# New place tables for a software-pipelined two-layer kernel on one core

## The chip, the core and the metric

The kernel runs on one core of a Trainium2 chip. TensorE (PE), VectorE (DVE), ScalarE (ACT) and GpSimd (POOL) each work through an instruction list of their own, in order; SyncE (SP) issues most DMAs. The metric is the device time of one execution in microseconds (us), lower is better. It is taken as the median of several executions.

## The reference, cut to what matters

The input is `x` of shape 8 x 512 x 128 in float32: eight batch elements ("batches") that don't depend on each other. Two layers follow each other.

```
xn = layernorm(x)
s  = attention(xn)                       # diagonal masked, softmax over 512
g  = silu(top-2-of-8 experts(xn))        # every expert: 128 -> 256 -> 128
x  = x + s * g
xn = layernorm(x)
s  = mamba(xn)                           # in_proj, conv of 4 taps, selective scan:
                                         #   16 states x 256 channels x 512 steps, out_proj, + xn
g  = silu(sublayer of the nearest of 8 centroids(xn))   # 128 -> 512 -> 128, relu
x  = x + s * g
```

## The kernel before, in words

**Groups of work.** The work of one batch is cut into steps of six groups, named by a letter, a name and a number:

- `A`: the first layer. `ln0`/`xn`/`xT` normalise and transpose; `gl` and `gate` choose the experts; `q k v s p o` are attention (`s0` to `s3` are the score tiles, `p0` to `p3` the transposed probabilities, `o0` to `o3` the outputs); `h0` to `h15` and `m0` to `m7` are the first and second products of the eight experts; `silu` ends the layer.
- `H`: the head of the second layer. `ln1`/`xm`, `hT`, `x1T`, `xi0/1`, `z0/1`, `u`, `bc` (with `bm`, `bl`, `cw`), `sc`, `al`, `rk`, `dl0/1`, `ln`, `du0/1`, and `put0` to `put3`, four indirect DMAs that sort the tokens by expert.
- `S`: the scan. It has 32 scans of 128 x 512 (16 states x 2 halves). `d` is the decay factor on ACT, `b` the spread of a row of B on PE, `scan` the product with B and the scan on DVE, `p` the product with C on POOL, `c` the load of a row of C. `a` adds the states of the first half on PE, `e` those of the second half on POOL (on PE for the last batch), `q` adds two states on DVE (line 1347).
- `F`: the experts of the second layer on eleven token tiles. `w` loads weights, `xs0` to `xs2` transpose, `h0` to `h10` and `y0` to `y10` are the two products, `st` stores, `get0` to `get3` gather back, `ft` and `silu` end it.
- `C`: the end of the batch: `y`, `op` (out_proj), `xr`, `out`.
- `P`: preparation of weights, once. `P pe 0` (lines 957 to 968) is 64 small matmuls.

**Which batch a step works on.** One iteration of the pipeline holds the 32 scans of one batch b. In the same iteration stand the `A` steps of batch b+2, the `H` steps of batch b+1, the `S` and `F` steps of batch b and the `C` steps of batch b-1 (`AHEAD`, line 360). The first layers of batches 0 and 1 and the head of batch 0 have no scans beside them: they fill the pipeline, and their places stand in a table of their own, `OWN` (lines 334 to 352).

**What sets the order.** No engine chooses. Each row of `ROWS` (line 66 on) is `(group, name, number, place, lag on ACT, lag on DVE, lag on POOL, PSUM bank)`. The place is a fraction of the iteration. `place` (line 370) adds the batch; `PLACES` and `ORDER` (lines 376, 377) sort all steps of all batches by it. `program` (line 380) gives each engine its list: PE and SP take the steps by place; ACT, DVE and POOL sort them by `floor(place * 32) + lag`. For DVE the scans are added at 0, 1, 2 ... 31 of their iteration. Steps in `OWN` have no lag. Each engine then runs those parts of a step that are its own.

**What ties the engines.** Semaphores, counted from `ORDER`. Those that matter here:

- `spread` (line 894): PE's `b_n` writes one of two PSUM rows, and waits for scan 2n-3; DVE's product for scan 2n waits for `b_n`, and stands in DVE's list ahead of scan 2n-1 (line 1375 on, `do`).
- Four PSUM banks (`work0` to `work3`) are shared by all products of `A`, `H`, `F` and `C`; `bank_free` (line 595) makes PE wait until the last user of the bank is read out.
- A scan writes one of five state buffers (`STATES`, line 44) and waits until its user before it is added up: in the first half by PE (`a`), in the second by POOL (`e`). `C y` (line 1349) waits for both sums.
- POOL's `get0` (line 1499 on) waits until the last store `st2` of `F` has landed. POOL's `ft` waits for ACT's `ft`.
- `cw` (line 687 on) stores the rows of C, after ACT's `bc`; SP stands still until then.
- ACT's `xn` needs the small POOL instructions of `ln0` (lines 1464 to 1467); PE's `xT` needs `xn`.

`a3`, `a7` and `a11` hold no instruction (their states are added in pairs).

Of the kernel before, what the change touches and what calls it, by code (L numbers as in the profile page):

```python
# [59 lines left out]
def group_tiles(k):  # L60
# [6 lines left out]
    ("P", "dve", 0, -4.19033, 0, 8, 3, None),  # L67
    ("P", "dve", 1, -2.47062, -4, 8, 3, None),
    ("P", "pe", 0, -1.67656, 0, 3, 3, None),
    ("P", "act", 0, -2.74339, 6, -2, -3, None),  # L70
    ("P", "dve", 2, -0.97742, -3, 8, -2, None),
    ("P", "dve", 3, -0.62565, -4, 8, 0, None),
    ("P", "dve", 4, -0.41210, -4, 8, 6, None),
    ("S", "d", 0, -0.06930, 2, -4, 8, None),
    ("S", "d", 1, -0.04250, 2, 4, 8, None),
    ("S", "b", 0, -0.04257, 4, 1, 1, None),
    ("C", "xr", 0, 0.10215, -2, 7, 0, None),
    ("A", "xin", 0, 0.00614, 6, 1, -3, None),
    ("F", "w", 0, 0.03213, -2, 7, 7, None),
    ("F", "xs", 0, 0.00000, 0, 4, -2, 1),  # L80
    ("S", "c", 0, 0.08107, 4, 7, -1, None),
    ("S", "c", 1, 0.10585, 3, 4, -1, None),
    ("F", "w", 1, 0.05645, -3, 0, 3, None),
    ("F", "h", 0, 0.03067, 0, 4, -4, 2),
    ("F", "w", 2, 0.11223, -3, 7, 6, None),
    ("F", "h", 1, 0.05851, 0, 0, -2, 3),
    ("F", "w", 3, 0.25246, 4, 8, 7, None),
    ("S", "d", 2, -0.00699, 1, 0, 8, None),
    ("S", "b", 1, 0.05502, 3, 0, 2, None),
    ("A", "xT", 0, 0.07492, -1, 3, 4, 0),  # L90
    ("S", "p", 0, 0.08069, 7, 8, -2, None),
    ("S", "d", 3, 0.00622, 0, 5, 8, None),
    ("A", "ln0", 0, 0.07442, 2, -3, -2, None),
    ("A", "xn", 0, 0.05034, -1, -3, 2, None),
    ("F", "ld", 1, 0.04079, -4, 0, -1, None),
    ("S", "c", 2, 0.11537, 5, -2, -2, None),
    ("A", "gl", 0, 0.08531, 0, 0, 7, 3),
    ("S", "p", 1, 0.08911, 5, 8, -2, None),
    ("S", "d", 4, 0.08095, -1, -1, 5, None),
    ("S", "b", 2, 0.08914, 4, 4, -4, None),  # L100
    ("C", "y", 0, 0.05655, -1, -1, -4, None),
    ("F", "w", 4, 0.25276, 0, 7, 8, None),
    ("F", "w", 5, 0.42886, -4, 7, 3, None),
    ("S", "p", 2, 0.10331, -2, 7, -1, None),
    ("S", "d", 5, 0.09590, -1, 3, 8, None),
    ("S", "e", 0, 0.10043, -4, -2, -2, None),
    ("A", "q", 0, 0.10060, -1, 4, -4, 0),
    ("C", "op", 0, 0.10037, -4, 0, 2, 1),
    ("A", "k", 0, 0.12863, 0, 6, 3, 3),
    ("A", "gate", 0, 0.10347, 2, 0, 7, None),  # L110
    ("F", "y", 0, 0.08472, 1, 5, 6, 2),
    ("S", "p", 3, 0.11413, 3, 8, -1, None),
    ("S", "d", 6, 0.11844, -1, 7, 7, None),
    ("S", "b", 3, 0.13684, 1, -2, -4, None),
    ("S", "a", 0, 0.06344, 2, -4, 5, None),
    ("F", "y", 1, 0.14612, 0, 3, 6, 3),
    ("C", "out", 0, 0.28650, 0, 8, 8, None),
    ("S", "c", 3, 0.22057, 5, 3, 2, None),
    ("F", "xs", 1, 0.02653, 0, 4, -3, 1),
    ("F", "h", 2, 0.14593, 0, -2, -1, 2),  # L120
    ("A", "s", 0, 0.14700, 0, -1, -2, 0),
    ("S", "p", 4, 0.15628, 1, 8, -3, None),
    ("S", "d", 7, 0.14633, 1, 3, 4, None),
    ("S", "e", 1, 0.15765, -4, -2, -2, None),
    ("F", "w", 6, 0.53888, -1, 7, 7, None),
    ("A", "s", 1, 0.15497, 2, 0, -3, 1),
    ("A", "gT", 0, 0.18211, 0, 6, 7, 2),
    ("A", "s", 2, 0.15828, 1, -1, -1, 3),
    ("A", "s", 3, 0.18212, 1, -1, 6, 0),
    ("S", "p", 5, 0.15952, 6, 8, -2, None),  # L130
    ("S", "d", 8, 0.18533, 1, 2, 6, None),
    ("S", "b", 4, 0.24697, 3, 3, -4, None),
    ("S", "a", 1, 0.13035, 0, -4, -1, None),
    ("A", "v", 0, 0.18227, -2, 1, -2, 2),
    ("A", "p", 0, 0.21815, 1, 7, -3, 1),
    ("F", "st", 0, 0.54576, 2, -1, 5, None),
    ("A", "p", 1, 0.22130, 1, 6, 2, 3),
    ("A", "p", 2, 0.22290, 1, 4, 0, 0),
    ("S", "p", 6, 0.19112, 4, 8, 0, None),
    ("S", "d", 9, 0.23616, 2, 3, 8, None),  # L140
    ("S", "e", 2, 0.25193, -4, -3, -1, None),
    ("S", "c", 4, 0.28439, 5, 6, 2, None),
    ("H", "ln1", 0, 0.25486, -1, 0, 0, None),
    ("H", "xm", 0, 0.33938, -1, -2, -3, None),
    ("A", "p", 3, 0.24715, 1, 4, 0, 2),
    ("A", "h", 0, 0.23766, 1, -4, -4, 1),
    ("A", "h", 1, 0.24707, 1, -1, 1, 0),
    ("S", "p", 7, 0.19307, -1, 8, 2, None),
    ("S", "d", 10, 0.25172, 1, -2, 7, None),
    ("S", "b", 5, 0.25269, 7, 8, 2, None),  # L150
    ("S", "a", 2, 0.20060, 0, -4, 3, None),
    ("F", "h", 3, 0.25384, 0, 3, -3, 3),
    ("F", "y", 2, 0.27707, 0, 7, 3, 0),
    ("A", "o", 0, 0.28591, -1, -3, -2, None),
    ("A", "o", 1, 0.31004, 4, 0, 7, None),
    ("A", "o", 2, 0.32685, 7, 2, 8, None),
    ("A", "o", 3, 0.34065, -1, 3, 1, 2),
    ("H", "hT", 0, 0.36348, 0, 6, 7, 2),
    ("S", "p", 8, 0.25598, 5, 8, 2, None),
    ("S", "d", 11, 0.28789, 0, -1, 7, None),  # L160
    ("S", "e", 3, 0.29700, -4, 0, 0, None),
    ("S", "c", 5, 0.35244, 7, 2, 5, None),
    ("A", "h", 2, 0.25171, 0, -1, -4, 0),
    ("A", "h", 3, 0.32603, -1, -2, -3, 3),
    ("S", "p", 9, 0.25913, 2, 7, 2, None),
    ("S", "d", 12, 0.33869, -1, 5, 3, None),
    ("S", "b", 6, 0.32732, 7, 4, -1, None),
    ("S", "a", 3, 0.39654, 6, -4, 2, None),
    ("A", "b2", 0, 0.25141, 0, 8, -3, 1),
    ("F", "h", 4, 0.27884, 1, -1, -4, 1),  # L170
    ("S", "p", 10, 0.32296, 6, 8, 3, None),
    ("S", "d", 13, 0.37771, -2, 7, 8, None),
    ("S", "e", 4, 0.33495, -4, -3, 0, None),
    ("H", "x1T", 0, 0.46354, -1, 7, -3, 1),
    ("A", "m", 0, 0.33671, 8, 1, 3, 0),
    ("S", "c", 6, 0.38581, 8, 4, 1, None),
    ("S", "p", 11, 0.36266, 5, 8, 2, None),
    ("S", "d", 14, 0.38317, -1, 5, 8, None),
    ("S", "b", 7, 0.35088, 6, 3, -1, None),
    ("S", "q", 4, 0.32753, 3, 1, 6, None),  # L180
    ("S", "a", 4, 0.39944, -1, -3, 6, None),
    ("A", "h", 4, 0.35391, 0, -4, -2, 1),
    ("A", "m", 1, 0.38008, 6, 1, -2, 1),
    ("A", "h", 5, 0.36890, 0, 0, 1, 0),
    ("A", "h", 6, 0.38782, -1, -3, -1, 0),
    ("F", "y", 3, 0.34764, 0, 5, 2, 3),
# [12 lines left out]
    ("S", "b", 8, 0.41835, 6, 5, 4, None),
    ("S", "a", 5, 0.47672, 3, -4, 0, None),  # L200
    ("F", "y", 4, 0.42082, 0, 5, 3, 0),
    ("H", "u", 0, 0.46438, -3, 0, -1, None),
    ("H", "z", 0, 0.52712, -1, 1, 3, 0),
    ("F", "ld", 2, 0.53904, -3, 4, -4, None),
    ("A", "h", 8, 0.50748, -2, 3, -2, 1),
    ("S", "p", 14, 0.43190, 4, 8, 2, None),
    ("S", "d", 17, 0.49706, -2, 0, 8, None),
    ("S", "e", 6, 0.51017, -4, 1, -3, None),
    ("F", "h", 6, 0.49976, -2, 1, -2, 0),
    ("H", "xi", 1, 0.47760, -2, 1, 4, 2),  # L210
# [12 lines left out]
    ("H", "u", 1, 0.53186, -2, 0, 8, None),
    ("A", "m", 3, 0.54082, 8, 2, 3, 1),
# [1380 lines left out]
```

## Time and profile before

| what | value |
|---|---|
| median of 3 executions | 950.92 us (949.97 to 953.21) |
| span of the profiled execution | 950.8 us, 15737 instructions; its device time is not listed apart from this span |
| busy: PE, DVE, ACT, POOL | 831.6, 798.4, 629.8, 604.9 us |
| weight loads of PE | 575.2 us |
| mean granted TensorE clock | 0.951 of full speed |
| first scan, last scan on DVE | start at 133.4 us, start at 932.7 us |

Busy time is the union of an engine's instructions. Matmul ends are modelled, so successive matmuls overlap a little in the rows. "Idle before" is the time in which the engine stood still ahead of an instruction, and the name behind the arrow is what ended it. The windows below are cut at the start of the first scan of each batch.

### The profile page before, as it was taken

How to read it: one execution, taken by the hardware profiler on the slowest of the kernel's cores; microseconds unless marked ns; L12 is line 12 of the kernel's file. 1: busy time of each engine (PE TensorE's matmuls, PEld its weight loads, DVE VectorE, ACT ScalarE, POOL GpSimd, SP SyncE). 2: the span in 40 equal slices, each digit the busy share in tenths (PEclk: the TensorE clock that was granted, in tenths of full speed). 3: DMA queues.
4: the chain of work that ended last, by engine and by line, in shares of the span. 5: the costliest groups of instructions: out<-in, count | busy, mean ns of one | idle time of the engine just before them, and what ended most of it. 6: DMA issues, size and time to landing. Idle time of an engine off the chain costs nothing.

```text
span 950.8 us, 15737 instructions
## 1 busy us (share of the span) xinstructions
PE 831.6 (87%) x4576; PEld 575.2 (61%) x4576; DVE 798.4 (84%) x1503; ACT 629.8 (66%) x1379; POOL 604.9 (64%) x556
## 2 busy tenths in 40 slices
PE   4989999998899879998799869998899876866885
PEld 2767666764677547765576547765676644543552
DVE  3352678999889998999989998899899999998994
ACT  2534667777687856776687866776686865684561
POOL 0000125769585884769585885769585888788664
PEclk9997999999899989999999999999899998886998
DMA  7200122232332333232331333232331333343441
GB/s 261 101 1 1 47 73 85 75 114 78 119 98 77 110 108 82 77 109 80 118 103 68 103 118 84 81 103 86 108 108 62 106 113 107 105 110 103 149 128 38
DMA packets 79430, 90.29 MB, mean 95 GB/s; under 512 B 8450, under 2 KB 49906, under 8 KB 78834
## 3 DMA queue, kind: packets, MB, share of 16 engines
q1 hardware_dynamic: 77298, 85.07, 29.4%
q0 software_dynamic: 2048, 4.20, 1.5%
q8 instruction: 40, 0.66, 0.3%
q14 instruction: 44, 0.36, 0.1%
HBM read 52.96 MB, written 13.04 MB: 69 GB/s over the span
## 4 chain that ended last, share of the span: by engine, by line
PE 39%; DVE 38%; issue 11%; POOL 6%; ACT 5%; SPq 1%; DVEq 0%; DMA 0%; POOLq 0%; ACTq 0%
DVE st L1341 13%; PE work L849 7%; PE work L855 6%; DVE acc L1225 4%; DVE b_row L1328 3%; PE work L890 3%; PE work L880 3%; PE work L778 3%; DVE cv L1254 3%; DVE dbu L1328 3%; POOL st L1518 2%; PE yacc L919 2%; DVE st L1347 2%; ACT prob L975 1%; PE work L769 1%
## 5 line engine op out<-in xcount | busy, mean ns | idle before, releaser
L1518 POOL TENSOR_TENSOR st<-st,Cs 128x512 f32<-128x512 f32 x249 | 320.0, 1297 | 158.0 <-DVE st L1341 152.8
L975 ACT ACTIVATE dA<-delta,Aneg 128x512 f32<-128x512 f32 x256 | 177.7, 718 | 12.9 <-DVE st L1341 12.8
L1341 DVE TENSOR_TENSOR_SCAN st<-dA,b_row 128x512 f32<-128x512 f32 x123 | 148.8, 1210 | 8.0 <-ACT dA L975 7.8
L1341 DVE TENSOR_TENSOR_SCAN st<-dA,dbu 128x512 f32<-128x512 f32 x128 | 154.6, 1208 | 0.0
L1525 POOL TENSOR_TENSOR y<-y,st 128x512 f32<-128x512 f32 x105 | 138.1, 1315 | 3.8
L849 PE MATMUL work<-xnT,w_w1a 128*128 128x512 f32 x256 | 132.7, 612 | 8.5 <-DVE delta L1309 7.0
L855 PEld LDWEIGHTS work<-w_w2a,hid 128*128 128x128 f32 x1024 | 125.1, 196 | 23.4 <-issue 8.7
L919 PE MATMUL yacc<-st,w_ident 128*128 128x512 f32 x208 | 115.7, 641 | 21.9 <-POOL st L1518 16.5
L975 ACT ACTIVATE hsT<-work,hs 128x128 f32<-128x128 f32 x352 | 100.2, 370 | 46.5 <-PE work L880 45.9
L855 PE MATMUL work<-w_w2a,hid 128*128 128x128 f32 x1024 | 128.8, 280 | 0.7 <-ACT hid L975 0.6
L880 PEld LDWEIGHTS work<-xsT,hs 128*128 128x128 f32 x704 | 98.6, 207 | 25.1 <-issue 5.9
L975 ACT ACTIVATE hid<-work,w_b1a 128x512 f32<-128x512 f32 x128 | 86.2, 683 | 37.6 <-PE work L849 33.3
L880 PE MATMUL work<-xsT,hs 128*128 128x128 f32 x704 | 103.2, 294 | 2.6 <-ACT ys L975 1.4
L1225 DVE SCALAR_TENSOR_TENSOR acc<-work,gates,acc 128x128 f32<-128x128 f32 x256 | 71.3, 340 | 35.2 <-PE work L855 32.8
L890 PE MATMUL work<-w_w2f,hsT 128*128 x704 | 99.2, 284 | 0.0
L1328 DVE TENSOR_TENSOR dbu<-b_row,du 128x512 f32<-128x512 f32 x123 | 85.1, 692 | 13.2 <-PE b_row L903 5.9
L890 PEld LDWEIGHTS work<-w_w2f,hsT 128*128 128x128 f32 x704 | 86.0, 192 | 5.7 <-issue 3.0
L1328 DVE TENSOR_TENSOR b_row<-b_row,du 128x512 f32<-128x512 f32 x123 | 84.0, 683 | 2.7
L849 PEld LDWEIGHTS work<-xnT,w_w1a 128*128 128x128 f32 x256 | 43.4, 192 | 42.3 <-issue 17.1
L919 PEld LDWEIGHTS yacc<-st,w_ident 128*128 128x128 f32 x208 | 37.0, 202 | 52.7 <-POOL st L1518 25.4
L1488 POOL DMA_INDIRECT xs_dram<-xn_tok,pos x32 | 32.2, 1006 | 57.6 <-DVE pos L1303 51.2
L903 PE MATMUL b_row<-bc,sel_b 96*128 96x512 bf16 x123 | 48.5, 394 | 21.9 <-DVE st L1341 21.9
(191 smaller groups left out, 1290.9 us busy)
## 6 DMA issues: line engine op xcount, KB each, us to landing
Cs<-c_dram SPq DMA_DIRECT2D x128, 256.0 KB, 3.6
hs<-w_w1f SPq DMA_DIRECT2D x88, 258.0 KB, 2.3
xs_in<-xs_dram SPq DMA_DIRECT2D x16, 256.0 KB, 3.4
ys_dram<-ys SPq DMA_DIRECT2D x16, 256.0 KB, 2.9
w_w1f<-in_w1f_dram SPq DMA_DIRECT2D x1, 2064.0 KB, 8.0
x_in<-in_x_dram SPq DMA_DIRECT2D x8, 256.0 KB, 5.6
w_w2f<-in_w2f_dram SPq DMA_DIRECT2D x1, 2048.0 KB, 12.4
kept_dram<-x_tok SPq DMA_DIRECT2D x8, 256.0 KB, 4.0
```

The lines of the kernel that those rows point to most:

```text
L849: last = mm(w[:], W["w1a"][:, i * 128:(i + 1) * 128], xnT[:], start=True, stop=True)
L855: last = mm(w[:, t * 128:(t + 1) * 128], hid[:, c % 4, t * 128:(t + 1) * 128], W["w2a"][:, c * 128:(c + 1) * 128], start=(c == PER * i), s ...
L880: last = mm(w[:, c * 128:(c + 1) * 128], w1s[:, i % 2, c * 128:(c + 1) * 128], xsT[:, i // 4 % 2, i % 4 * 128:(i % 4 + 1) * 128], start=Tr ...
L890: last = mm(r, hsT[:, i % 2, c * 128:(c + 1) * 128], W["w2f"][:, bass.ds(e * H1 + c * 128, 128)], start=False, stop=(c == HC - 1))
L903: mm(rows_bank(n, b)[:], row_of(n), bc3[:, par], start=True, stop=True).then_inc(sig["B_in"], 1)
L919: mm(yacc[:], ident[:], state(s), start=False, stop=(n == NS - 1)).then_inc(sig["y_sum0"], 1)
L975: return nc.scalar.activation(out, in_, func, **k)
L1225: last = V.scalar_tensor_tensor(acc[:, t], w[:, t * 128:(t + 1) * 128], gates[:, t, i:i + 1], acc[:, t], ALU.mult, ALU.add)
L1328: V.tensor_tensor((dbu0, rows_bank(n, b))[h][:], rows_bank(n, b)[:], du[:, par, h], ALU.mult).then_inc(sig["dBu"], 1)
L1341: V.tensor_tensor_scan(state(s), dA[:, s % DECAYS], (dbu0, rows_bank(n, b))[h][:], 0.0, ALU.mult, ALU.add).then_inc(sig["scan"], 1)
L1518: G.tensor_tensor(state(s), state(s), Cs[:, b.of(NS, n) % C_BUFS], ALU.mult).then_inc(sig["P"], 1)
L1525: G.tensor_tensor(y1[:], y1[:], state(s), ALU.add).then_inc(sig["y_sum1"], 1)
```

## The change

No instruction is added, removed or altered. The places of `ROWS`, its lags and banks, and the tables `OWN` and `OWN_BANKS` have new values. `AHEAD`, `LAG`, `STATES` and all code stay. The diff replaces nearly every row; here are the rows that are spoken of below.

```diff
 ROWS = [
-    ("P", "pe", 0, -1.67656, 0, 3, 3, None),
+    ("P", "pe", 0, -1.91080, 0, 3, 3, None),
...
-    ("F", "xs", 0, 0.00000, 0, 4, -2, 1),
+    ("F", "xs", 0, -0.11627, -2, 4, -2, 3),
...
-    ("F", "h", 0, 0.03067, 0, 4, -4, 2),
+    ("F", "h", 0, -0.02332, 0, 4, -4, 0),
...
-    ("A", "xT", 0, 0.07492, -1, 3, 4, 0),
+    ("A", "xT", 0, -0.00752, 1, 3, 4, 3),
...
-    ("A", "ln0", 0, 0.07442, 2, -3, -2, None),
-    ("A", "xn", 0, 0.05034, -1, -3, 2, None),
+    ("A", "ln0", 0, 0.02507, 2, -10, -5, None),
+    ("A", "xn", 0, -0.07075, 2, -3, 2, None),
...
-    ("C", "y", 0, 0.05655, -1, -1, -4, None),
+    ("C", "y", 0, 0.04106, -1, 0, -4, None),
...
-    ("S", "d", 9, 0.23616, 2, 3, 8, None),
+    ("S", "d", 9, 0.25211, -1, 3, 8, None),
...
-    ("A", "m", 0, 0.33671, 8, 1, 3, 0),
+    ("A", "m", 0, 0.35005, 8, -1, 3, 2),
...
-    ("S", "c", 10, 0.67012, 7, 8, 2, None),
+    ("S", "c", 10, 0.57540, 7, 8, 2, None),
...
-    ("H", "cw", 0, 0.77328, 4, 7, -4, None),
+    ("H", "cw", 0, 0.44605, 4, 7, -4, None),
...
-    ("F", "get", 0, 0.83381, 4, 6, 2, None),
+    ("F", "get", 0, 0.78844, 4, 6, 1, None),
...
-    ("F", "get", 3, 0.88365, 0, 8, 2, None),
+    ("F", "get", 3, 0.93264, 0, 8, 2, None),
...
-    ("A", "m", 7, 0.95782, 8, 0, 4, 3),
+    ("A", "m", 7, 0.97159, 8, -1, 4, 2),
...
 OWN = {
     ("A", 0): (
-        -2.47358, -4.12153, -4.15752, -4.47547, -3.96000, -3.84171, -3.57697, -3.77930, -3.40151, -3.32920, -3.31868, -3.31571,
+        -4.73497, -6.29962, -9.23557, -6.95863, -5.61949, -4.96893, -4.95574, -4.56186, -4.38585, -4.36247, -3.73522, -3.37503,
...
 OWN_BANKS = {
```

What the tables make of the engines' lists, in an iteration in the middle, around the change of batch (the batch is given as an offset from the one whose scans run; the instructions are the same):

```
PE before:   b15 h12..h14(+2) a12 h15(+2) a13 m6(+2) | b0 m7(+1) a14(-1) xs0 a15(-1) xs1 Fh0 b1 Fh1 a0 xT(+2) y0 gl(+2) b2 op(-1) ...
PE after:    b15 h13(+2) xs0(+1) m6(+2) h14 h15(+2) a13 m7(+2) Fh0(+1) | b0 xT(+2) a14 a15(-1) b1 Fh1 y0 b2 gl(+2) xs1 op(-1) ...
DVE before:  scan27 q12 du0 du1 scan28 al scan29 scan30 m6 m7 scan31 ln0(+3) | scan0 silu(+1) Cy(-1) scan1 scan2 ...
DVE after:   scan22 ln0(+3) ... q12 scan27 du0 du1 scan28 m6 scan29 scan30 m7 scan31 | scan0 silu(+1) scan1 Cy(-1) scan2 ...
POOL before: e12 p27 e13 get0 du0 du1 get1 get2 get3 p28 p29 p30 p31 ft e14 e15 ln0(+3) | p0 ...
POOL after:  e12 get0 get1 ln0(+3) get2 du0 du1 p27 p28 e13 p29 p30 e14 get3 p31 e15 ft | p0 ...
SP before:   ... st1 w10 cw c12 c13 c14 st2 c15
SP after:    ... w8 cw c10 xin(+3) c11 keep w9 w10 st1 c12 c13 w0(+1) c14 w1(+1) fetch st2 ld1(+1) c15
```

Further in the iteration: PE before has `b5 Fh3 y2 Fh4 o0 o1 h3 o2 b6 m0`, after it has `b5 y2 Fh4 y3 h2 o0 b6 h3 m0`. DVE before takes `m0` after scan 11, after the change it takes it after scan 10. ACT before has `d8 p0 p1 p2 h0 h1 p3 b2 h2 Fh3 y2 d9`, after it has `p0 p1 h1 d8 p2 d9 Fh3 b2`.

In the fill (batches 0 and 1), ahead of the first `b0` on PE, the list now also holds `h15` and `m6` of batch 1 and `xs0` and `h0` of `F`, 0.86 to 1.79 us each in the rows below. DVE's `ln1` of batch 0 now stands ahead of `gl` and `gate` of batch 1, and ACT's `xm` of batch 0 ahead of the score tiles `s0` to `s3` of batch 1.

## Rows read from the trace of the kernel before

**Rows 1.** The page: span, busy time by engine, and two groups of DVE.
```profile
span 950.8 us, 15737 instructions
PE 831.6 (87%) x4576; PEld 575.2 (61%) x4576; DVE 798.4 (84%) x1503; ACT 629.8 (66%) x1379; POOL 604.9 (64%) x556
...
L1341 DVE TENSOR_TENSOR_SCAN st<-dA,b_row 128x512 f32<-128x512 f32 x123 | 148.8, 1210 | 8.0 <-ACT dA L975 7.8
...
L1328 DVE TENSOR_TENSOR b_row<-b_row,du 128x512 f32<-128x512 f32 x123 | 84.0, 683 | 2.7
```

**Rows 2.** Windows from first scan to first scan: length, busy, clock, DMA.
```profile
0.00:133.42 133.42, 115.78 (x611) 81.09 (x611) 60.25 (x206) 64.71 (x123) 14.45 (x28) 0.95 0.23 76
133.42:239.04 105.62, 97.78 (x562) 67.40 (x560) 97.01 (x188) 79.04 (x175) 72.52 (x67) 0.98 0.32 97
...
345.79:454.74 108.95, 99.87 (x560) 70.01 (x560) 97.94 (x185) 78.17 (x172) 78.30 (x72) 0.95 0.32 94
...
669.60:774.93 105.33, 97.32 (x560) 69.25 (x560) 96.89 (x177) 77.53 (x172) 77.00 (x71) 0.97 0.30 92
774.93:867.31 92.38, 64.70 (x299) 41.67 (x299) 86.48 (x123) 56.45 (x128) 73.92 (x67) 0.82 0.37 106
867.31:950.80 83.49, 64.53 (x308) 40.42 (x306) 65.77 (x79) 39.34 (x98) 53.93 (x43) 0.93 0.37 113
```

**Rows 3.** Waits of DVE, 239.04 to 774.93 us: us, times, longest.
```profile
DVE gm L1196 <- PE work L748: 6.2, 5, 2.2
DVE st L1341 <- ACT dA L975: 5.4, 5, 1.1
DVE dbu L1328 <- PE b_row L903: 4.0, 5, 0.8
DVE acc L1225 <- PE work L855: 3.7, 7, 1.3
```

**Rows 4.** Timeline around the first scan of batch 3, at 454.74 us.
```profile
445.26 0.99 POOL L1505 DMA_INDIRECT fe<-ys_dram,pos  x1 [0.16 <-issue]
...
448.77 4.96 POOL L1518 TENSOR_TENSOR st<-st,Cs 128x512 f32<-128x512 f32 x4
...
456.14 0.66 PE L873 MATMUL work<-w_ident,xs_in 128*128 128x128 f32 x4 [2.46 <-ACT xsT L975]
...
457.53 0.20 POOL L1464 TENSOR_TENSOR ve<-mv,eps 128x4 f32<-128x4 f32 x1
```

**Rows 5.** Chain of waits, three PE steps: start, us (h of F; h; m).
```profile
486.02 0.89 PE work L880 x8
...
488.70 0.86 PE work L849 x2
...
490.67 1.79 PE work L855 x16
```

**Rows 6.** Timeline of the fill, 57 to 90 us.
```profile
62.41 1.03 PE L748 MATMUL work<-w_gate,xnT 128*128 128x8 f32 x8 [2.09 <-ACT xnT L975]
...
69.70 11.55 PE L964 MATMUL yacc<-w_betaT,w_w1f 128*128 128x1 f32 x64
...
84.03 0.69 ACT L975 ACTIVATE prob<-work,nmax 128x512 f32<-128x512 f32 x1 [12.11 <-DVE nmax L1192]
```

**Rows 7.** Timeline of DVE after the first scan of batch 7.
```profile
870.47 0.69 DVE L1353 TENSOR_TENSOR du<-yacc,zg 128x512 f32<-128x512 f32 x1 [1.95 <-PE yacc L919]
873.30 0.76 DVE L1357 SCALAR_TENSOR_TENSOR yacc<-u,w_dskip,y 128x512 f32<-128x512 f32 x1 [2.14 <-POOL y L1525]
```

**Rows 8.** Timeline of the tail, after the last scan's start at 932.73 us.
```profile
933.50 4.92 POOL L1518 TENSOR_TENSOR st<-st,Cs 128x512 f32<-128x512 f32 x4
...
939.56 0.69 DVE L1353 TENSOR_TENSOR du<-yacc,zg 128x512 f32<-128x512 f32 x1 [5.64 <-PE yacc L919]
```

**Rows 9.** The page's DMA issues: KB each, us to landing.
```profile
Cs<-c_dram SPq DMA_DIRECT2D x128, 256.0 KB, 3.6
...
ys_dram<-ys SPq DMA_DIRECT2D x16, 256.0 KB, 2.9
```

More of the change, by code:

```diff
@@ L335 @@
     ("A", 0): (
[4 rows of a table removed]
[4 rows of a table added]
     ),
     ("H", 0): (
-        -1.74095, -1.65846, -1.52697, -1.49484, -1.52111, -1.40608, -1.44055, -1.37873, -1.37265, -1.27871, -1.21166, -0.93890,
-        -1.08660, -1.03498, -1.03373, -1.59445, -1.09880, -0.94857, -0.45437, -0.80556, -0.88318, -1.36857, -1.23008, -0.51530,
-        -0.38577, -0.84495, -0.80927, -1.47192,
+        -2.00817, -1.85312, -1.74054, -1.49763, -1.52849, -1.32934, -1.11521, -1.29887, -0.68391, -1.17544, -1.20930, -0.29698,
+        -0.99788, -0.77916, -0.95986, -1.96195, -1.01357, -0.64233, -0.33350, -0.65780, -0.39694, -1.76661, -1.75366, -0.22585,
+        -0.12009, -1.21719, -5.11900, -3.61250,
     ),
     ("A", 1): (
[4 rows of a table removed]
[4 rows of a table added]
     ),
```

522 rows, old and new, of tables (OWN, OWN_BANKS, ROWS) are left out of this document.

## The prediction

> **What bounds the kernel now.** The page first [rows 1]: PE is busy 87% of the 950.8 us, DVE 84%, and neither is full. The windows by iteration [rows 2] show three stages. The fill, 133.4 us, ends at the first scan and is PE's: after its first matmul (10.6 us) PE has 122.8 us and is busy 115.8. Then come six iterations of 105.3 to 109.0 us (106.9 on average: 641.5 us from 133.42 to 774.93), in which DVE and PE each work 95 to 100 us. Then two lighter ones, 92.4 and 83.5 us, in which DVE has the scans and little else.
>
> In the six, DVE's busy time is 97 to 98 us and the iteration is 9 us longer. So the reader should ask what DVE waits for [rows 3]: over five iterations 6.2 us for `gl`, 5.4 us for a decay factor of ACT, 4.0 us for a B row, 3.7 us for expert products: 19.3 us, or 3.9 each iteration. The other 5 us are pauses between its own dependent instructions and waits under 0.6 us; new places shift them but don't remove them.
>
> Where PE's lateness comes from is seen at the change of batch [rows 4]. POOL still has two gathers and four products with C to do there (to 453.7 us), and gets to `ln0` of batch b+3 only at 457.5 us. PE stands 2.46 us ahead of `xs1`, since the one bank is read out by ACT only after ACT's waits for POOL. `xT` and `gl` come last, and from there PE's string (attention, `h`, up to `m0`) is as long as DVE's work beside it. So two engines alternate: PE sets the pace in the first third, DVE in the rest.
>
> **The change, part by part.** The work is the same; only what stands where counts. I went through the new lists by hand, segment by segment between two `b` steps on PE and the scans that they feed on DVE, with the durations of the rows.
>
> 1. *The fill.* Ahead of the first `b0` now also stand `h15` 0.86, `m6` 1.79, `h0` of `F` 0.89 us [rows 5] and `xs0` (half of that, 0.45): 4.0 us. They are gone from behind it, so they cost the end nothing; the cover is PE's own list, which is full on both sides. PE's standstills there are 122.8 - 115.8 = 7.0 us [rows 2]. The new order puts ACT's `xT` of batch 1 ahead of `silu` (most of the 2.09 us [rows 6]). The long preparation of 11.55 us on PE [rows 6] held DVE and with it ACT (12.11 us), behind which `xm` of batch 0 stood; now `xm` runs beside it, and `hT` can follow at once. The bounds are 0 (another wait takes the place) and 7.0 us; I take 2.5, the one wait plus a little, as the rest of PE's list was dense anyway. First scan at about 133.4 + 4.0 - 2.5 = 135 us.
>
> 2. *Six changes of batch.* `ln0` moves from behind scan 31 to behind scan 22 and on POOL ahead of the last products, so `xT` is ready when `b0` is; `xs0`, `h0`, `m7` move ahead of `b0`. This takes away the wait for `gl`, 6.2 / 5 = 1.2 us. `d9` moves ahead of three ACT steps: 5.4 / 5 = 1.1 us. Ahead of `b6` stand six steps instead of seven, four of them new: 4.0 / 5 = 0.8. Of the expert products' 0.7 us I take 0.4. Together 3.5 us. Against it, new waits: `m0` is now wanted by DVE one scan earlier (1.89 us at most by [rows 1], 1.21 + 0.68) while PE has it after about the same work; I take 0.7. `C y` needs POOL's last sum, which now has four gathers and `ln0` ahead of it, but stands a scan later: 0.6. Net 3.5 - 1.3 = 2.2 us; bounds: 3.9 (all of [rows 3], nothing new) and a loss, below. Six times 2.2 is 13 us.
>
> 3. *The last change of batch.* Here DVE is light and POOL is late: 1.95 + 2.14 us of DVE ahead of and inside `C y` [rows 7]. `C y` moves behind scan 1, which is ready: that fills 1.9 us; POOL's `ft` (one of the 1.3 us kind, as a product is 4.96 / 4 = 1.24 [rows 4]) moves behind the sum: 1.2 us. I take 3; bounds 1.9 and 4.1.
>
> 4. *The tail.* Four gathers stood ahead of four products, which ended at 938.4 us [rows 8]. Now three gathers stand ahead of `p27` and one between `p30` and `p31`. POOL's total is the same, so the last product ends only where it did, but the sums of `p28` to `p30` no longer bunch up on PE behind it, and the last gather lands later. I take 1.8 us; bounds -1.3 (the gather, one POOL step later, sets the end) and 5.6 (all of DVE's wait).
>
> 5. *Edits with one answer.* `al` moves an iteration on: its value is read by ACT's `ft` behind the next change of batch, no wait. `a3`, `a7`, `a11` are empty. `xin`, `keep`, `xr`, `out` pass other SP steps but are wanted half an iteration later. The banks: I looked for each PE step at the last user of its bank. The close pairs are `xs0` behind `du0` and `m6` behind `xs0` (bank 3); they cost PE about 1 us where it then waits for POOL anyway. `c10` stands behind `cw` and so behind `bc`: it lands 3.6 us later [rows 9], perhaps 2.5 us after `p20` could start; POOL has 78 us of work in 107 [rows 2] and waits for `put0`'s positions next, so nothing. If that cover is gone, it is up to 2.5 us an iteration.
>
> Sum: 2.5 + 13 + 3 + 1.8 = 20.3 us, 950.8 - 20.3 = 930.5. The span of the profiled execution and the median (950.92) agree within 0.1 us, so I predict 931 us.
>
> **Rivals.**
>
> *A. POOL sets the change of batch (slower).* `get0` now stands ahead of `du0`, `p27` and all that follows, and waits for a store that takes 2.9 us to land [rows 9]; SP issues it behind `w1` and `fetch`. After it POOL has three gathers at 1.3 us (0.99 + 0.3 [rows 4]) and `ln0` at 2.3 us (457.53 to 459.8): 2.9 + 3.9 + 2.3 = 9.1 us after `y10`, before it can multiply the `du` that DVE has finished after about 5.3. Then eleven 1.25 us steps up to the last sum. DVE has scans 28 to 31, 0, `m6`, `m7`, `silu` in front of scan 1, about 13 us, and scan 1 needs POOL's sum `e14` as its buffer. If `y10` is out no earlier than DVE's `du`, DVE waits 1.1 us before scan 1 and 2.1 more before `C y`; with 1.6 at `m0` and 1.2 at `xs0` and `c10` the new waits are 6.0 against the 3.5 removed: +2.5, six times 15, less what fill and tail give (4.3): 961 us. It decides where the new waits pass 3.5 + 7.3 / 6 = 4.7 us an iteration. For it: POOL is the engine that is late in [rows 4] and [rows 7]. Against: in my walk `y10` is out 2 to 3 us earlier than that, since it stands ahead of `b14` on PE and DVE's `du` behind scan 27.
>
> *B. The waits only move (same).* DVE's busy time sets the iteration: PE's steps pass from one side of `b0` to the other, and DVE waits elsewhere for what is now behind. Then nothing is won in the six, and ends and fill give 2 to 3 in all: 948 us. For it: four waits of about 1 us each [rows 3] are the sort that a shifted order makes anew. Against: 2.46 us of PE and `ln0` on POOL are a real queue, not a shift.
> The Trainium skill has a rule that speaks for this rival (Perfetto Trace Analysis, Identifying the Most-Contended Engine): take the engine of the highest occupancy and optimise that first, and don't read PE's matmul occupancy that way. By it DVE (84%) is the bound, moving PE's steps wins nothing, and the time is rival B's. The same page (Optimization Strategy) also allows for regimes with different engines, which is how the windows read.
>
> *C. All waits close (much faster).* The 3.9 us of [rows 3] go and nothing comes: 6 x 3.9 = 23, plus 2.5 + 3 + 1.8, and PE's fill gains some more: 920 us, down to 915 if the fill gives all 7.
>
> *D. The lists hardly differ where it matters*, so that no time moves: the lists in the change section speak against it.
>
> **How the numbers follow.** The forecast has 0.50 (924 to 940), C 0.16, B 0.15, A 0.16, D 0.03. About 0.3% (2.9 us) is what a measurement of this kernel can tell from no change. Faster by more: all of the forecast and C, and two thirds of B: 0.76. Within: the rest of B and D: 0.08. Slower: A, 0.16. The range takes in C's bulk and B, and leaves A's main part and C's end out: 916 to 953.
>
> **What the profile will show.** Right: first scan at 134 to 136 us; the first six first-scan distances at 103 to 106 us, DVE's busy time in them unchanged at 98; no wait of `gm` for PE line 748 and none of the scan for `dA`; POOL's line 1464 some 20 us ahead of the first scan of its iteration; no 2.46 us ahead of `xs1`; DVE's wait in `C y` of batch 6 under 1.5 us. Wrong, towards A: DVE waits for POOL `y` (line 1525) ahead of line 1341 or 1357 in each iteration, and POOL waits ahead of line 1505 for the store. Towards B: distances at 107 with DVE waiting for line 855 or 763 instead. A first scan later than 137 us would show the fill's step wrong. DVE's busy time up by several us would be a cause that I haven't counted.

## The result, and the profile after

The change makes the kernel slower: 965.12 us (median of 10 runs) against 953.46 us for the kernel before, measured beside it; the ratio is 1.0112, with a 95% interval of 1.0088 to 1.0137. Forecast were 931 us and a range of 916 to 953, so the change went the other way and the time lies outside the range. The profiled execution has a span of 963.3 us, 12.5 more than before [rows 1].

The page of the kernel after: the span, busy time by engine, and the same groups of DVE as in [rows 1].

```profile
span 963.3 us, 15737 instructions
PE 838.7 (87%) x4576; PEld 580.5 (60%) x4576; DVE 822.1 (85%) x1503; ACT 630.0 (65%) x1379; POOL 605.3 (63%) x556
...
L1341 DVE TENSOR_TENSOR_SCAN st<-dA,b_row 128x512 f32<-128x512 f32 x123 | 148.8, 1210 | 0.6 <-PE work L927 0.3
...
L1328 DVE TENSOR_TENSOR b_row<-b_row,du 128x512 f32<-128x512 f32 x123 | 84.1, 684 | 4.5 <-DVE bc L1272 0.5
```

The instructions are the same in number on every engine, POOL's busy time is the same, and the scans take 1210 ns as before. But DVE is busy 822.1 us and not 798.4: 23.7 us more, for the same work. That is what the prediction had called "a cause that I haven't counted".

The windows from first scan to first scan of the kernel after, to set against [rows 2] (start and end, then length, busy time of PE, PEld, DVE, ACT, POOL, clock, DMA):

```profile
0.00:134.40 134.40, 118.50 (x637) 84.66 (x638) 61.31 (x210) 67.71 (x130) 15.63 (x30) 0.95 0.25 83
134.40:240.73 106.33, 94.52 (x548) 65.27 (x547) 98.68 (x181) 79.33 (x174) 70.10 (x66) 1.00 0.30 92
...
351.21:461.14 109.93, 99.26 (x561) 69.69 (x562) 102.47 (x185) 78.37 (x172) 78.14 (x72) 0.97 0.30 94
...
681.53:790.11 108.58, 99.62 (x566) 68.71 (x567) 100.69 (x178) 75.88 (x167) 78.48 (x69) 0.98 0.31 96
790.11:884.21 94.10, 65.08 (x298) 42.91 (x297) 86.89 (x123) 57.52 (x129) 74.45 (x67) 0.83 0.33 102
884.21:963.30 79.09, 63.77 (x295) 40.56 (x293) 66.44 (x81) 36.87 (x92) 53.51 (x43) 0.91 0.33 105
```

The first scan comes 1.0 us later. The six iterations take 790.11 - 134.40 = 655.7 us instead of 641.5: +14.2. Batch 6 takes 1.7 more, the last stretch 4.4 less. In the six DVE is busy 607.4 us in all (up to 102.5 in one), where it was 585.9 (up to 98.1). POOL's busy time there and the clock are as before; PE's is 4.7 us more (591.4 against 586.6), but its idle time grew too, from 54.9 to 64.4.

DVE's waits over five iterations of the kernel after, to set against [rows 3] (us, times, longest):

```profile
DVE acc L1225 <- PE work L855: 11.7, 5, 2.4
DVE st L1341 <- ACT dA L975: 3.7, 5, 0.7
DVE work L1365 <- PE work L936: 1.9, 2, 1.3
```

The waits for `gl` (line 1196) and for a B row of PE are gone from the list, as forecast, and that for a decay factor is smaller. `m0` waits 2.3 us in each iteration, more than the 0.7 taken. Yet DVE's idle time in the six fell from 55.6 to 48.3 us (the six lengths less DVE's busy time in them): the loss is not in DVE's waits, it is inside its instructions. The next rows show which. They are DVE and POOL in the middle of batch 3, around `sc` (start us, duration us), first before, then after.

```profile
513.56 1.28 POOL L1518 TENSOR_TENSOR st<-st,Cs 128x512 f32<-128x512 f32 x1 [1.35 <-DVE st L1341]
...
515.66 0.19 DVE L1171 TENSOR_TENSOR eq<-eq,w_first 128x32 f32<-128x32 f32 x1
...
516.11 0.19 DVE L1173 TENSOR_TENSOR ohr<-eq,gr 128x32 f32<-128x32 f32 x1
...
516.44 0.18 DVE L1280 CAST ohb<-ohr 128x32 bf16<-128x32 f32 x1
...
518.49 1.27 POOL L1518 TENSOR_TENSOR st<-st,Cs 128x512 f32<-128x512 f32 x1 [3.65 <-DVE st L1341]
```

```profile
525.50 1.28 POOL L1525 TENSOR_TENSOR y<-y,st 128x512 f32<-128x512 f32 x1
...
526.01 0.19 DVE L1170 TENSOR_TENSOR eq<-work,am 128x32 f32<-128x32 f32 x1
526.24 0.59 DVE L1171 TENSOR_TENSOR eq<-eq,w_first 128x32 f32<-128x32 f32 x1
526.73 1.27 POOL L1518 TENSOR_TENSOR st<-st,Cs 128x512 f32<-128x512 f32 x1
526.86 0.19 DVE L1172 TENSOR_REDUCE gr<-eq 128x4 f32<-128x32 f32 x1
527.08 0.97 DVE L1173 TENSOR_TENSOR ohr<-eq,gr 128x32 f32<-128x32 f32 x1
...
527.96 1.27 POOL L1525 TENSOR_TENSOR y<-y,st 128x512 f32<-128x512 f32 x1
...
528.20 1.07 DVE L1280 CAST ohb<-ohr 128x32 bf16<-128x32 f32 x1
```

Before, `sc` runs between two products of POOL, and its instructions take 0.19 us. After, it stands right behind scan 18, where POOL runs three instructions end to end. Line 1171 starts at 526.24 and ends at 526.83, 0.05 us behind POOL's instruction; 1173 ends at 528.05, again 0.05 us behind POOL's next (528.00); 1280 ends at 529.27, POOL's third at 529.23. They are instructions of 32 elements that wait, inside their own recorded time, for POOL's to end. Line 1170 (one operand in PSUM) and line 1172 (a reduction) run beside the same instructions in 0.19 us. So this depends on operands: lines 1171 and 1173 read two tensors from SBUF, 1280 is a cast from SBUF to SBUF.

The Trainium skill states this (SBUF — State Buffer, Who interferes with whom): GpSimd's only ports are one pair that it shares with VectorE, as an exclusive lock for a whole instruction; a VectorE instruction with two SBUF inputs needs it against a GpSimd instruction that reads SBUF, a cast may need it too, a reduction never does. What the trace can show of this agrees: the two-input lines and the cast took 0.59, 0.97 and 1.07 us against 0.19, the reduction 0.19 in both kernels. It can't show the ports, nor what a GpSimd instruction that only writes would do.

Summed over all executions, the lines that grew most are 1280 (1.4 to 7.7 us), 1173 (3.1 to 8.5), 1170 and 1206 in `gate` (1.5 to 5.9, 2.4 to 6.8), 1316 in F's `silu` (5.3 to 9.0), 1301 in `rk` (1.5 to 4.5) and 1171 (3.1 to 5.8). Some stood beside POOL before and shrank: 1347, the sum of two states, from 28.2 to 23.0, and 1292, a scan of eight elements in `rk`, from 4.3 to 1.4. So the kernel before had this contention too, only less of it.

### The profile page after: what moved, and what is told of

It reads as the page before. It is cut to its first block, busy times and chain, and to the rows that moved or that the text cites. A ratio compares the mean times of both kernels' runs of the same rounds, so it can differ in the third digit from the quotient of the medians.

```text
span 963.3 us, 15737 instructions
## 1 busy us (share of the span) xinstructions
PE 838.7 (87%) x4576; PEld 580.5 (60%) x4576; DVE 822.1 (85%) x1503; ACT 630.0 (65%) x1379; POOL 605.3 (63%) x556
## 3 DMA queue, kind: packets, MB, share of 16 engines
q1 hardware_dynamic: 77298, 85.07, 28.2%
## 4 chain that ended last, share of the span: by engine, by line
DVE 43%; PE 29%; issue 17%; POOL 5%; ACT 4%; SPq 1%; DMA 1%; DVEq 0%; POOLq 0%
DVE st L1341 15%; PE work L849 5%; PE work L855 5%; DVE acc L1225 4%; DVE dbu L1328 3%; DVE b_row L1328 3%; POOL st L1518 3%; PE work L778 2%; PE work L880 2%; PE work L890 2%; PE work L936 2%; DVE cv L1254 1%; PE yacc L919 1%; PE work L762 1%; PE yacc L964 1%
## 5 line engine op out<-in xcount | busy, mean ns | idle before, releaser
L1518 POOL TENSOR_TENSOR st<-st,Cs 128x512 f32<-128x512 f32 x249 | 323.7, 1307 | 184.1 <-DVE st L1341 174.1
L1341 DVE TENSOR_TENSOR_SCAN st<-dA,dbu 128x512 f32<-128x512 f32 x128 | 154.9, 1210 | 4.7 <-ACT dA L975 4.5
L1341 DVE TENSOR_TENSOR_SCAN st<-dA,b_row 128x512 f32<-128x512 f32 x123 | 148.8, 1210 | 0.6 <-PE work L927 0.3
L855 PEld LDWEIGHTS work<-w_w2a,hid 128*128 128x128 f32 x1024 | 122.5, 192 | 24.0 <-issue 14.4
L1525 POOL TENSOR_TENSOR y<-y,st 128x512 f32<-128x512 f32 x105 | 133.8, 1274 | 3.6
L849 PE MATMUL work<-xnT,w_w1a 128*128 128x512 f32 x256 | 130.2, 603 | 5.9 <-DVE zg L1261 3.2
L855 PE MATMUL work<-w_w2a,hid 128*128 128x128 f32 x1024 | 125.8, 276 | 4.2 <-issue 4.1
L880 PEld LDWEIGHTS work<-xsT,hs 128*128 128x128 f32 x704 | 94.6, 202 | 32.6 <-issue 10.3
L880 PE MATMUL work<-xsT,hs 128*128 128x128 f32 x704 | 99.8, 287 | 8.4 <-DMA hs<-w_w1f 4.8
L890 PE MATMUL work<-w_w2f,hsT 128*128 x704 | 102.3, 290 | 0.0
L890 PEld LDWEIGHTS work<-w_w2f,hsT 128*128 128x128 f32 x704 | 88.8, 198 | 12.5 <-issue 10.7
```

What stands on the lines that cost most here:

```text
L849: last = mm(w[:], W["w1a"][:, i * 128:(i + 1) * 128], xnT[:], start=True, stop=True)
L855: last = mm(w[:, t * 128:(t + 1) * 128], hid[:, c % 4, t * 128:(t + 1) * 128], W["w2a"][:, c * 128:(c + 1) * 128], start=(c == PER * i), s ...
L880: last = mm(w[:, c * 128:(c + 1) * 128], w1s[:, i % 2, c * 128:(c + 1) * 128], xsT[:, i // 4 % 2, i % 4 * 128:(i % 4 + 1) * 128], start=Tr ...
L890: last = mm(r, hsT[:, i % 2, c * 128:(c + 1) * 128], W["w2f"][:, bass.ds(e * H1 + c * 128, 128)], start=False, stop=(c == HC - 1))
L1341: V.tensor_tensor_scan(state(s), dA[:, s % DECAYS], (dbu0, rows_bank(n, b))[h][:], 0.0, ALU.mult, ALU.add).then_inc(sig["scan"], 1)
L1518: G.tensor_tensor(state(s), state(s), Cs[:, b.of(NS, n) % C_BUFS], ALU.mult).then_inc(sig["P"], 1)
```

## The experiments

Three theories stood against each other. **S**: contention at SBUF lengthens DVE's steps. **W**: a wait took the place of those removed, `m0`'s above all. **P**: POOL's new order at the change of batch sets the time. All runs stand beside the kernel before on the same chip (medians of 952.9 to 953.6). The kernel after, at 965.1, was not measured again beside them; run 8 has a kernel that differs from it by one place and took 964.25.

### 1. The contention given to the kernel before

`sc` of DVE moved from ahead of scan 18 to behind it, nothing else:

```
- ... scan 17, z 0, u 1, sc, scan 18, z 1, scan 19
+ ... scan 17, z 0, u 1, scan 18, sc, z 1, scan 19
```

> The kernel before, with one step of VectorE's list moved: the scorer `sc` stands behind scan 18 instead of ahead of it, where POOL's product 18 and an add of y run beside it. Theory S (VectorE and POOL stand in each other's way at SBUF: an instruction of VectorE that reads two operands from SBUF, or a cast from SBUF to SBUF, waits until POOL's instruction ends): lines 1171, 1173 and 1280, 0.19 us each in the kernel before, come to 0.6 to 1.1 us each, sc grows from 1.1 to between 2.1 and 3.4 us in 7 batches, and the time grows by 7 to 16 us, to 960 to 969. Theory W (the waits moved, as m0 on PE): nothing is late for sc, so the time stays within 3 us of 953. Theory P (POOL sets the changes of batch, which this doesn't touch): within 3 us of 953 too.

958.8 us, ratio 1.0043 (1.0022 to 1.0065). Slower, by less than expected (7 to 16). Line 1173 rose as it should, to the same 966 ns (executions, then min/median/max in ns):

```profile
L1173 DVE TENSOR_TENSOR ohr<-eq,gr x8: 191/966/968, 101.1 to 831.1; 128x32 f32<-128x32 f32 x8
```

Line 1171 rose too (3.1 to 9.5 us in all), but the cast did not (POOL's instructions had ended), and line 1347, which had stood beside POOL, fell by 5.2: DVE's busy time is 804.3, +5.9. In the profile the six iterations grew by 2.9 us only, 5.2 came in batch 6, where DVE's idle time rose, and the last stretch was 2.0 shorter. So this run shows the lengthening at will, and only weakly what it costs.

### 2. The contention taken from the kernel after, by its operands

```
-                    first_max(g, wl, am, eq, ohr)
+                    first_max(g, wl, am, wl, ohr)
...
-                    V.tensor_copy(ohb[:], ohr[:]).then_inc(sig["hot"], 1)
+                    V.tensor_reduce(ohb[:], ohr[:].unsqueeze(3), AX.X, ALU.max).then_inc(sig["hot"], 1)
```

The mask is kept in the PSUM bank of the scores (`wl`), and the cast is a reduction over an axis of length one.

> The kernel after, with the same order on every engine: the scorer `sc` keeps its mask in its own PSUM bank instead of in SBUF (so that lines 1171 and 1173 have one operand in SBUF), and its cast to bf16 is written as a reduction over an axis of length one, an instruction that did not stretch anywhere in the two traces. Theory S: sc falls from 3.45 to about 1.2 us beside the same products of POOL, VectorE's busy time by 14 to 16 us, and the time from 965 to 949 to 953. Theories W and P: the durations of sc may fall or not, but the time stays within 3 us of 965, since what they hold for the loss (the wait of m0, the order of POOL at the change of batch) is unchanged.

950.06 us, ratio 0.9967 (0.9944 to 0.9991): 15 us less than the kernel after. In the profile, lines 1173 and 1280 stand in the same places beside POOL and no longer stretch:

```profile
L1173 DVE TENSOR_TENSOR ohr<-work,gr x8: 191/191/192, 94.2 to 828.4; 128x32 f32<-128x32 f32 x8
...
L1280 DVE TENSOR_REDUCE ohb<-ohr x8: 186/186/187, 94.5 to 828.8; 128x32 bf16<-128x32 f32 x8
```

DVE's busy time is 803.1, 19.0 less than in the kernel after. S holds; W and P had 965. But not every microsecond came straight back. Of the 16.0 us between the two profiled spans, 9.0 stand in the six iterations, where DVE's idle time rose from 48.3 to 56.3 us, and 3.7 ahead of the first scan, where no line had stretched in either kernel. That part the contention doesn't explain: with this same fill the first scan comes at anything from 130.6 to 134.9 us in the traces of these runs.

### 3. The same two lines in the kernel before

> The control to the last edit: the same two edits of `sc` (mask in its PSUM bank, cast as a reduction), in the kernel before, where sc stood clear of POOL and its lines 1171, 1173 and 1280 already took 0.19 us. Theory S (contention at SBUF was what the edit took away from the kernel after): sc stays at 1.1 us and the time within 2 us of 953. If the edit is good by itself, whatever POOL does (a cheaper form, an earlier bank): 938 to 948.

953.62 us, ratio 1.0008 (0.9967 to 1.0048). The edit is worth nothing where `sc` stands clear of POOL, so the gain in the kernel after is not the form's (to within the interval, some 4 us).

### 4. The contention taken away from POOL's side

The kernel after, with the product 18 and the additions 7 and 8 left out on POOL in the first seven batches (those parts of `y` are then missing), and DVE untouched:

```
+                if s == 18 and not b.is_(NB - 1):
+                    pool.wait_ge(sig["P"], b.of(STEPS, s))
+                    pool.sem_inc(sig["P"], 1)
...
+                if n not in (0, 7, 8):
                     G.tensor_tensor(y1[:], y1[:], state(s), ALU.add).then_inc(sig["y_sum1"], 1)
```

> The kernel after with VectorE's code and order as they are; POOL leaves out the product 18 and the additions 7 and 8 of y in the first seven batches (part of y is then missing), which are the three instructions that ran beside `sc`. Theory S: lines 1171, 1173 and 1280 of sc fall to 0.19 us with no change to them, sc from 3.45 to 1.1 us, and the time to 947 to 953, as when sc's own operands were moved. If it is the order of VectorE's list or PE that costs and sc's length is only a symptom: 960 to 966.

949.89 us, ratio 0.9963 (0.9936 to 0.9990), as in run 2, and the cast itself, unchanged in the code, is short:

```profile
L1280 DVE CAST ohb<-ohr x8: 180/181/182, 94.6 to 827.1; 128x32 bf16<-128x32 f32 x8
```

This edit also takes 28.8 us of work off POOL (605.3 to 576.5), so by itself it could not tell the overlap from a shorter POOL list. But run 2 leaves POOL's work alone, and the two give the same time within 0.2 us. For `sc` the cause is shown from both sides.

### 5. The gate, on DVE alone

> The kernel after, with scan 3, C op, gate in the order of the kernel before (after has C op, scan 3, gate). Theory S: gate's lines 1206 and 1170 stood at 1.07 and 0.92 us beside POOL's product 3 and add 0; behind C op the product has ended, so they fall to 0.19 unless POOL's addition of xr (which C op releases) takes its place; 5 batches by 1.6 us is 8 us at most: 957 to 962. Theory W: only the wait of 0.6 us ahead of C op is covered by scan 3: 5 times 0.6 is 3 us, 962, with the lines as they were. Theory P: C op comes later, so POOL's and ScalarE's steps behind it come later: 965 to 970.

970.38 us, ratio 1.0182 (1.0141 to 1.0222): rather a loss (the profiled execution is the fastest of its six, 964.46), and the gate's lines still stretched. The timeline of this run, around the gate in batch 3, says why:

```profile
473.56 1.27 POOL L1542 TENSOR_TENSOR ot<-ot,xr 128x512 f32<-128x512 f32 x1 [2.63 <-DVE ot L1368]
...
474.02 0.86 DVE L1204 SCALAR_TENSOR_TENSOR eq<-gt,w_first 128x32 f32<-128x32 f32 x1 [0.54 <-ACT gp L975]
...
474.78 1.28 POOL L1518 TENSOR_TENSOR st<-st,Cs 128x512 f32<-128x512 f32 x1
...
475.13 0.97 DVE L1206 TENSOR_TENSOR oh<-eq,gr 128x32 f32<-128x32 f32 x1
```

POOL's list in the kernel after has C's addition ahead of product 3, so `C op` of DVE releases both of them just as the gate begins. The overlap is set by both lists; moving one engine's step moved it onto another of POOL's. The expectation had named this case, but gave it no price, and S's 957 to 962 is missed. P had 965 to 970, since `C op` and what POOL does behind it come later. This run doesn't refute that; run 6, in which it comes later still and P had 950 to 955, does.

### 6. The gate, on both engines

To run 2 are added the places of the kernel before: DVE has scan 3, `C op`, `gate`, and POOL

```
- p 0, p 1, p 2, C op, p 3, e 0, e 1, p 4, p 5
+ p 0, p 1, p 2, p 3, e 0, p 4, e 1, C op, p 5
```

> The kernel after with `sc` in PSUM (950) and, beside it, the gate as the kernel before has it on both engines: VectorE scan 3, C op, gate; POOL has the addition 1 of y and C op's addition of xr behind product 4, so nothing of POOL's follows product 3 while gate runs. Theory S: gate's lines 1206 and 1170 fall from 1.07 and 0.92 to 0.19 us in five or six batches, 1.6 us each, up to 9 us: if VectorE still set the pace 942. But `m0` now waits 3.6 us for PE, so PE may take up most of it: 944 to 950. Theory P (POOL's order ahead of the products sets the time): C op's addition comes later, slower, 950 to 955.

943.1 us, ratio 0.9878 (0.9815 to 0.9942): 7 less than run 2, and faster than both kernels. The gate runs in a gap of POOL's:

```profile
461.93 1.27 POOL L1518 TENSOR_TENSOR st<-st,Cs 128x512 f32<-128x512 f32 x1 [1.31 <-DVE st L1341]
...
464.15 0.19 DVE L1206 TENSOR_TENSOR oh<-eq,gr 128x32 f32<-128x32 f32 x1
...
464.83 0.19 DVE L1170 TENSOR_TENSOR eq<-gt,gm 128x32 f32<-128x32 f32 x1
...
471.79 1.27 POOL L1518 TENSOR_TENSOR st<-st,Cs 128x512 f32<-128x512 f32 x1 [8.59 <-DVE st L1341]
```

DVE's busy time is 795.2, 3.2 under that of the kernel before, and the rest of the new places, without what `sc` and `gate` lost, is worth 953.6 - 943.1, some 10 us. By the two traces 2.9 of them lie in the six iterations and 3.6 in the last stretch.

### 7. Places alone

The kernel after with nothing of its code changed: the gate's places as in run 6, and on DVE `u 1, m 3, sc` in the place of `sc, u 1, m 3`.

> The kernel after with nothing of its code changed, only places: the gate's arrangement of the run before (VectorE scan 3, C op, gate; POOL's addition 1 and C op's addition behind product 4), and on VectorE u 1, m 3, sc in the place of sc, u 1, m 3, so that sc begins when POOL's product 18 is ending. Theory S: gate gives 1.6 us in five or six batches, sc some 2 us less beside POOL but 0.9 us of waiting for m 3 on PE, so 1.1 us in six: 965 less 9 less 7 is 949, range 946 to 955, still short of the 943 of the run with sc in PSUM. If contention were not the cause: 962 to 968.

960.26 us, ratio 1.0059 (1.0032 to 1.0085). The added contention is gone (DVE is busy 797.4 us, as in the kernel before), but only 5 of the 16 us forecast came: in the six DVE's idle time is 67.9 us, where it was 48.3. PE has a new wait in its place (us, times, longest, over four iterations):

```profile
PE work L880 <- DVEq L1279: 6.9, 4, 1.7
```

Line 1279 is the step of DVE that hands back the bank of `sc`. Two steps later on DVE, the bank comes back later, and PE's next step in it, `h` of F, stands 1.7 us. I had priced the wait for `m3` and not the bank. Six such waits are 10.4 us, and the six iterations take 650.4 us, 11.8 more than in run 6. That fits, but no run took this wait away alone. So what a stretched instruction costs depends on what stands ready to take its place.

### 8. DVE's and PE's waits

`m0` moved back behind scan 11, in the kernel after and then in that of run 6:

> The kernel after, with `m0` of VectorE back behind scan 11, where it stood in the kernel before. It waits 2.33 us for PE in six iterations. Theory W: that wait is the loss, and it goes: 6 by 2.3 is 14 us, 951. Theory S: the wait goes too, but it stood in the place of other waits (VectorE's idle time is less in after than in before), so part of it comes back a step or two later: 955 to 962, and VectorE's busy time stays at 822. Theory P: 965.

966.73 us, ratio 1.0136 (1.0096 to 1.0175): no gain. W had 951, and S's 955 to 962 is missed too; only P's 965 is near. The wait for line 855 is 9.8 us in four iterations, where it was 9.4: now it is other `m` steps that wait. DVE's busy time rose by 4.5 us, most of it in line 1347 (23.0 to 27.0), so the move made an overlap of its own.

> The same, with `m0` of VectorE behind scan 11 as in the kernel before. With sc short, VectorE's wait for m0 is 3.6 us in each of the six iterations. Theory W, now that contention no longer covers it: scan 11 fills the wait, 6 by 1.8 is 11 us less than without it, 935 to 940. Theory PE (the pace in these iterations is set by PE, whose h and m steps come in the same order): the wait turns up at another step, within 2 us of the run without it.

946.1 us, ratio 0.9916 (0.9893 to 0.9939): no gain here either. W falls, with and without contention.

`s 0` and `s 1` of DVE behind scan 4, in the kernel of run 6, and then `silu` of F behind `gl` as well:

> The kernel of 943 us with s 0 and s 1 of VectorE behind scan 4. With the gate short, VectorE waited 1.5 us there for the scores of s 0 and s 1 from PE; scan 4 takes 1.8 us and covers it. If VectorE sets the pace (theory S with VectorE as the bound): 6 by 1.3 us less, 935 to 938. If PE sets the pace of these iterations now, the wait turns up elsewhere: 941 to 945.

> The same, with F silu of VectorE (line 1316, two operands in SBUF, 0.67 us alone, up to 1.77 beside POOL's product 2) behind gl, so that most of product 2 has run. Theory S: line 1316 falls from 6.9 to about 5.5 us in all, 1 to 2 us less than without it if VectorE sets the pace; otherwise within 2 us of it.

945.04 (ratio 0.9916; 0.9881 to 0.9951) and 942.68 us (0.9883; 0.9843 to 0.9923): both within their intervals of run 6. So VectorE alone doesn't set the pace there, as S had it. Line 1316 did not fall in the second (9.5 us in all, 8.5 in the first).

PE stands 2.4 us ahead of `b2` in each change of batch after the change, for scan 1. The place of `b2` behind `gl`, `a3` and `xs1`, in the kernel of run 6 and in the kernel after:

```
-    ("S", "b", 2, 0.05621, 4, 4, -4, None),
+    ("S", "b", 2, 0.07500, 4, 4, -4, None),
```

> The kernel of 943 us (sc in PSUM, gate as before) with one place changed: PE's `b2` stands behind gl, a 3 and xs 1 instead of ahead of them. PE stood 2.4 us there in each change of batch for VectorE's scan 1. Theory Q (once contention is gone, PE's wait at the change of batch is what holds the six iterations; it took the place of the wait ahead of xs 1 in the kernel before): gl and xs 1 (2.8 us) fill that wait, 6 by 1.5 to 2.4 us less, 929 to 935. Theory N (no single engine's wait holds them, the loop over both does): within 2 us of 943.

> The same one place of `b2` in the kernel after as it is, with sc and gate beside POOL. Theory S: VectorE is then busy 102 of 110 us in an iteration and sets the pace, so an earlier gl gives at most what VectorE waits for PE there (1.0 and 0.6 us at F silu and C op): 959 to 965, and VectorE's busy time stays near 822. If PE's wait at the change of batch were the loss all along, and contention only beside it: 945 to 952.

942.91 (ratio 0.9908; 0.9877 to 0.9938) and 964.25 us (1.0136; 1.0091 to 1.0180). Both unchanged. In the first, the wait is now ahead of C's product, over four iterations:

```profile
PE work L936 <- DVE du L1360: 9.9, 5, 2.6
```

### 9. POOL at the change of batch

> The kernel with sc in PSUM and the gate as before (943), and on POOL the four gathers together behind du, ahead of product 27, where the kernel after has get 0 to 2 ahead of du and get 3 after product 30. Theory P (POOL's order at the change of batch sets what VectorE can do there): du comes 3 us earlier, which gives up to 3 us in six changes, 925 to 935; or the gathers ahead of the products hold them up, and it is slower by as much, 950 to 960. Theory S: VectorE waits for nothing of POOL's there, within 3 us of 943.

960.31 us, ratio 1.0074 (1.0045 to 1.0104): 17 us more than run 6. Here the wait that rival A named does appear, ahead of the scans (over four iterations):

```profile
DVE st L1341 <- POOL y L1525: 7.0, 4, 1.9
```

So POOL's order there can cost what A said, and more: the six iterations grew by 8 us and batch 6 by 7.7. But the kernel after has its gathers on both sides of the products, and no wait of this kind among DVE's largest. P is a real mechanism, and nothing in the trace of the kernel after shows that this change sets it off.

## Why the prediction was wrong

- **The step that failed is step 2**, by its premise more than by its terms: DVE's work was taken to cost the same wherever it stands ("DVE's busy time in them unchanged at 98"). It costs 101 on average, and up to 102.5. The six iterations were forecast 13 us shorter and came 14.2 longer. With `sc` and `gate` freed of POOL (run 6) they take 770.5 - 131.9 = 638.6 us, 2.9 less than before. So 17 of the 27 us of error in this stage went with the contention; by places alone (run 7, 650.4 us) only 5 did. The walk through the lists looked at what each step waits for, never at what runs beside it on POOL.
- **The other 10 us of step 2** stay without contention: the listed waits went, but new ones came for nearly all of it. One reading was wrong: ahead of `b6` PE has five steps and not six, and two of them are new (`y3`, `h2`), not four. `m0` waits 2.3 us, where all waits for the `m` products together were 0.7 an iteration, and PE has 2.4 us ahead of `a15` and 2.4 ahead of `b2` at the change of batch, in the place of the 2.46 ahead of `xs1` [rows 4]. This is rival B's mechanism. Moving single waits on DVE (`m0`, `s0`) or on PE (`b2`) gave nothing, so no single one holds the iteration. What does was not settled: a loop over DVE's scans, POOL's products and PE's sums fits the rows, but is only argued.
- **Step 1** forecast the first scan at about 135; it came at 134.40. But the sum counted 2.5 us of gain for it, holding the 4.0 us moved ahead as saved further back. They are not seen there: batch 6 is 1.7 us longer. Nor does one trace settle 2.5 us: the first scan comes at 130.6 to 134.9 us in the traces with the fill of the kernel after, and at 133.4 to 135.5 in those with the fill of the kernel before.
- **Steps 3 and 4** forecast 4.8 us from the last change of batch and the tail; the last stretch is 4.4 us shorter (79.1 against 83.5). Right in sum, and DVE's idle time ahead of line 1353 fell as the steps had it, from 8.5 to 2.3 us in all.
- **The base** was 950.8 us, and the kernel before took 953.46 when measured beside the kernel after: 2.7 us that don't touch the sign.
- **Step 5** named banks and waits, with one answer each: no change of the time was traced to them. Run 7 shows how near they are: a bank given back two steps later cost PE 1.7 us an iteration.
- **Rival A** had the right sign and nearly the time (961) for the wrong reason: none of DVE's larger waits is for POOL's sums. The way POOL did slow DVE is not a wait that a view of waits shows.
- The profile of before had the sign of it: line 1206 took 1.06 us in one of its eight executions, and line 1347 took 1.18 us on average, 0.67 at the least and 4.00 at the most.

## What to carry to other kernels

When a step of VectorE is moved, look at what GpSimd runs beside its new place, and at its operands: two in SBUF, or a cast within SBUF, waited here for a whole GpSimd instruction, or for several end to end, and that shows as a longer instruction and not as a wait. Compare the busy time of each engine before and after first; if it rises for the same instructions, compare min, median and max by line. Here the operand was the better cure (the scores' own PSUM bank, 15 us) and the place the worse one (5 us), since the operand leaves the order alone. Then measure: time won back on one engine can turn into waits, as it did in runs 2 and 7.

## What the hardware showed that I had not expected

- A comparison of 128x32 elements took 0.19 us alone and up to 1.07 us beside a POOL instruction of 1.27 us. The scans of 128x512 (1.21 us, one operand in PSUM) and the reductions of 128x32 (0.19 us) never grew. A scan can: line 1292, with both operands in SBUF, took 0.17 us alone and up to 1.07 beside POOL in the kernel before:

```profile
L1292 DVE TENSOR_TENSOR_SCAN endt<-ones,ntile x8: 174/508/1067, 103.9 to 834.0; 128x8 f32<-128x8 f32 x8
```

- One instruction can lose more than one of POOL's. In the kernel before a sum of two states (0.67 us at the least) took 4.00 us, while POOL ran three instructions end to end, and the kernel after has one of 4.17. Why it didn't get in between them, as the small ones above did, is not shown:

```profile
849.87 2.48 POOL L1518 TENSOR_TENSOR st<-st,Cs 128x512 f32<-128x512 f32 x2
...
851.34 4.00 DVE L1347 TENSOR_TENSOR st<-st 128x512 f32<-128x512 f32 x1
...
852.32 1.25 POOL L1525 TENSOR_TENSOR y<-y,st 128x512 f32<-128x512 f32 x1
853.54 1.25 POOL L1518 TENSOR_TENSOR st<-st,Cs 128x512 f32<-128x512 f32 x1
```

- It works the other way too. In the kernel after POOL's product took 1.74 us instead of 1.27 where VectorE's line 1316, with both operands in SBUF, had started just ahead of it:

```profile
471.45 0.69 DVE L1316 SCALAR_TENSOR_TENSOR ys<-ys,fe 128x512 f32<-128x512 f32 x1 [1.01 <-ACT ys L975]
...
471.53 1.74 POOL L1518 TENSOR_TENSOR st<-st,Cs 128x512 f32<-128x512 f32 x1
```

- A cast of 128x32 from f32 to bf16 took 1.07 us beside POOL, and 0.186 us written as a reduction over an axis of length one.
